# A two-layer transformer kernel on one core: routing by a search for the two largest, routing of the second step done earlier, and the first chain of layer 1 out of PSUM

## What is computed

```python
x = L0_attn_x                                  # (16, 256, 128)
xn = layernorm(x)
x = x + attn0(xn) + ffn0(xn)
xn = layernorm(x)
x = x + attn1(xn) + ffn1(xn)

def attn0(x):     # 8 heads of 64, windows of 128 and their neighbours
    xn = layernorm(x) * ln_g + ln_b
    qk, v = split(xn @ w_qkv.T)                # keys and queries are the same
    q, k = rotate(bucket(qk)), rotate(look_around(bucket(qk)))
    return softmax(mask(q @ k.T)) @ look_around(bucket(v)) @ w_out.T

def ffn0(x):      # a shared expert and 8 routed ones of 256, 2 per token
    p = softmax(x @ router_w + router_b)
    topk_probs, topk_idx = top_k(p, 2)
    weights = scatter(topk_idx, topk_probs)
    mixed = sum_e weights[:, e] * (gelu(x @ rw1[e] + rb1[e]) @ rw2[e] + rb2[e])
    return gelu(x @ sw1 + sb1) @ sw2 + sb2 + mixed

def attn1(x):     # gated unit without softmax, over the whole sequence
    u, v, base = split(silu((layernorm(x) * ln_w + ln_b) @ uv_w.T + uv_b))
    q, k = rope(base * gamma[0] + beta[0]), rope(base * gamma[1] + beta[1])
    return (u * (relu(q @ k.T / sqrt(128) + bias) ** 2 @ v)) @ o_w.T + o_b

def ffn1(x):      # a shared expert and routed ones
    return routed(x, 8 of 32 experts of 64, out of the best 2 of 4 groups) + shared(x)
```

## Time and profile before

| | before |
|---|---|
| median of 3 runs | 1052.2 us |
| lowest and highest | 1051.57 and 1052.24 us |
| profiled execution, its own time | 1052.27 us |
| span of the profile | 1051.0 us |
| TensorE busy | 997.6 us |
| VectorE, ScalarE, POOL busy | 680.0, 506.6, 425.9 us |
| mean granted TensorE clock | 0.99 of full |

### The profile page before, as it was taken

How to read it: one execution, slowest core, us unless ns; L and a number is a source line. 1 busy time by engine, 2 the same in 40 slices (tenths; PEclk the granted TensorE clock), 3 DMA queues, 4 the chain that set the end, 5 groups by cost and what they waited for, 6 DMA issues and landing times.

```text
span 1051.0 us, 13320 instructions
## 1 busy us (share of the span) xinstructions
PE 997.6 (95%) x4440; PEld 623.3 (59%) x4440; DVE 680.0 (65%) x1501; ACT 506.6 (48%) x1192; POOL 425.9 (41%) x336
## 2 busy tenths in 40 slices
PE   5799889799999999999999999999999999999998
PEld 2455556367555666556665675656665566656655
DVE  4846755849766587647766497665976557724933
ACT  3463573252654546454474525635266453644222
POOL 4737315454036520655108350175303652044433
PEclk9899989999999999999999999999999999999999
DMA  7140220060232302332032310323022220242061
GB/s 263 29 144 1 93 60 1 6 147 21 70 86 71 80 1 92 84 82 49 11 108 59 90 41 11 121 65 89 21 89 67 68 73 8 84 104 80 21 143 40
DMA packets 34565, 72.78 MB, mean 69 GB/s; under 512 B 4545, under 2 KB 5313, under 8 KB 34113
## 3 DMA queue, kind: packets, MB, share of 16 engines
q1 hardware_dynamic: 33072, 69.03, 24.0%
q10 hardware_dynamic: 1424, 2.90, 0.8%
HBM read 69.04 MB, written 2.88 MB: 68 GB/s over the span
## 4 chain that ended last, share of the span: by engine, by line
PE 88%; DVE 6%; issue 3%; ACT 3%; DMA 0%; POOL 0%; DVEq 0%; ACTq 0%; POOLq 0%
PE ps L692 11%; PE ps L589 11%; PE ps L453 9%; PE ps L455 9%; PE ps L454 9%; PE ps L501 6%; PE ps L514 6%; PE ps L526 5%; PE ps L667 3%; PE ps L477 3%; PE ps L484 2%; PE ps L597 2%; PE ps L638 2%; PE ps L448 1%; PE ps L493 1%
## 5 line engine op out<-in xcount | busy, mean ns | idle before, releaser
L1091 ACT ACTIVATE wide<-ps 128x512 f32<-128x512 f32 x136 | 80.9, 595 | 221.4 <-PE ps L455 220.8
L1022 ACT ACTIVATE pw<-ps,w_cols 128x512 f32<-128x512 f32 x144 | 98.8, 687 | 111.2 <-PE ps L455 109.5
L1771 POOL TENSOR_TENSOR atc<-atc,wide 128x512 f32<-128x512 f32 x64 | 82.8, 1294 | 156.4 <-DVE atc L1519 156.4
L982 ACT ACTIVATE pw<-ps,nmax 128x256 f32<-128x256 f32 x256 | 118.1, 470 | 52.8 <-DVE nmax L1319 52.7
L589 PE MATMUL ps<-pw,w_w 128*128 128x512 f32 x288 | 138.1, 603 | 0.0
L1753 POOL TENSOR_TENSOR kr<-qks,w_rope 128x512 f32<-128x512 f32 x32 | 43.5, 1360 | 194.8 <-DVE qks L1299 194.8
L1328 DVE COPY pt<-ps 128x512 f32<-128x512 f32 x128 | 85.7, 681 | 32.7 <-PE ps L514 31.7
L1390 DVE SCALAR_TENSOR_TENSOR pt<-ps,w_cols,wb 128x512 f32<-128x512 f32 x64 | 47.8, 747 | 88.0 <-PE ps L589 73.6
L514 PE MATMUL ps<-ident,pw 128*128 128x128 f32 x512 | 83.7, 287 | 21.3 <-DVE pt L1328 13.1
L1319 DVE TENSOR_REDUCE nmax<-ps 128x4 f32<-128x1024 f32 (+1 forms) x80 | 79.3, 1009 | 36.0 <-PE ps L501 35.9
L514 PEld LDWEIGHTS ps<-ident,pw 128*128 128x128 f32 x512 | 55.9, 142 | 60.9 <-issue 39.9
(11 more groups left out here) (221 smaller groups left out, 2098.3 us busy)
## 6 DMA issues: line engine op xcount, KB each, us to landing
wb<-scratch SPq DMA_DIRECT2D x128, 256.0 KB, 4.0
wb<-scratch SPq DMA_DIRECT2D x32, 512.0 KB, 5.4
wide<-scratch SPq DMA_DIRECT2D x16, 512.0 KB, 6.0
xin<-in_x SPq DMA_DIRECT2D x8, 256.0 KB, 2.7
out<-wide SPq DMA_DIRECT2D x8, 256.0 KB, 2.1
w_w<-in_w ACTq DMA_DIRECT2D x1, 1152.0 KB, 11.0
wb<-in_w SPq DMA_DIRECT2D x1, 1152.0 KB, 12.4
w_ed<-in_ed SPq DMA_DIRECT2D x1, 1024.0 KB, 17.3
```

The costliest lines, as they stand in the source:

```text
L982: m = act.activation(pw[:, u % 2, j, :], ps[:, score_bank(u, par), qt * SEQ:(qt + 1) * SEQ], ACT.Exp, bias=nmax[:, u % 3, j:j + 1], scale= ...
L1022: act.activation(hid[:, n % 4, :], bank(UPS0[n % 2]), ACT.Gelu, bias=cols[:, C_B1 + 2 * e + c:C_B1 + 2 * e + c + 1], scale=1.0).then_inc(* ...
L1771: pool.tensor_tensor(hh[h], hh[h], sgl[:, (c + 1) % 3, :], ALU.mult).then_inc(*HH_POOL.one)
```

## The change

1. **Search instead of rank.** `route0_top` takes the place of `route0_rank`: one `max` per tile (the 8 logits in falling order, `top0`), a memset that overwrites places 2 to 7 with a number no logit has, and one `match_replace` per tile, which marks the two places that hold the two largest. `route0_less` takes the maximum from `top0`, so its own reduction goes. `zc` is no longer scratch; the waits of the rank and of `z1_cols(0)` for it go. In step 0 the search stands behind round 1 of the attention, `route0_less` behind round 2, `exp0` and `route0_weights` in round 4, and the turning of the weights in round 5 or 6.
2. **The second step's routing one step early.** In `experts0(0)`, `y0_rows(1)`, `turn_y0(1)`, `y0_high(1)`, `y0_low(1)` and `logits0(1)` stand some calls earlier, so the logits come before `attention_out` and the search before `join0`. Two buffers `yc` make this possible: `columns0` and `columns1` choose one by step. At the head of `attention(1)`, `rows0(0)` on TensorE and `x1_rows(0)` and `variance1(0)` on VectorE move from before round 0 to its end, into a score bank; `shifts(1, 0)` moves to round 2, `z1_rows(0)` behind both exponentials of round 3.
3. **First chain out of PSUM.** `affine1(0)` writes to PSUM banks 6 and 2 (`affine`) and stands behind the gelus of the shared expert and of the first; `swap1` and `rope1_add` read there. In `experts0_and_chain1(1)` the order changes on all engines: the statistics of x of step 2 (`variance0(2)`, `shifts(0, 2)`, `power(0, 2)`) come earlier, `qk1` one expert's product later, `tanh1` before a gelu and not after `z0_cols`, the routing of layer 1 ahead of the rotation of step 2, the last two projections later.
4. **Key halves on POOL.** A new event `ROPED_K` for the key half. In step 2 the four adds of the key half are done by POOL (`rope_add_k`), not by VectorE.
5. **Start.** ScalarE makes `short_ident` as soon as `ident` is there (`IDENT`), where POOL did; so ScalarE's first activation no longer stands behind the first shift.

The steps from 2 on keep their order on all engines, but for the search in the place of the rank in `experts1`.

```diff
@@ buffers, banks
-        y0c, y1c = sb("y0c", [P, 2, TOK], F32R), sb("y1c", [P, 2, TOK], F32R)
+        yc = [sb("yc0", [P, 2, TOK], F32R), sb("yc1", [P, 2, TOK], F32R)]
...
+        def affine(s, i):
+
+            return qa1[:, i, :] if s else bank((6, 2)[i])
+
+        def columns0(s):
+
+            return yc[0 if s == 0 else 1]
+
+        def columns1(s):
+
+            return yc[1 if s == LAST else 0]
@@ pe_program, attention
-                if second:
-                    rows0(0, 7)
...
+                    if u == 0 and second:
+                        rows0(0, score_bank(0, 1))
...
-                    if u == 4 and first:
-                        turn_weights0(s, score_bank(4, 1))
+                    if u == 5 and first:
+                        turn_weights0(s, score_bank(5, 1))
@@ pe_program, experts0
+                if s == 0:
+                    turn_y0(n, 6)
                 down0(s, 5)
                 up0(s, 7)
                 if more:
-                    values(n, 1, 6)
-                    values(n, 2, 3)
+                    values(n, 1, 3)
+                    values(n, 2, 2)
+                if s == 0:
+                    logits0(n, 6)
                 down0(s, 6)
                 if more:
-                    values(n, 3, 6)
-                if s == 0:
-                    turn_y0(n, 2)
+                    values(n, 3, 3)
                 attention_out(s)
                 if s == 0:
-                    logits0(n, 3)
+                    turn_logits0(n, 6)
                     scores(n, 0)
                 down0(s, 7)
                 if s == 0:
-                    turn_logits0(n, 6)
                     scores(n, 1)
@@ pe_program, experts0_and_chain1
                 up0(s, 1)
+                down0(s, 0)
                 turn_y1(x, 3)
-                down0(s, 0)
+                up0(s, 2)
                 qk1(x, 0, 6)
                 qk1(x, 1, 2)
-                up0(s, 2)
@@ act_program, attention
                     v1_silu(0, 1)
-                    affine1(0)
                     gelu(s, E0)
                     gelu_half(s, 0, 0)
...
                 gelu_half(s, 0, 1)
+                if second:
+                    affine1(0)
@@ act_program, before the first step
-            w.wait_ge(*CONSTANTS.at(0))
+            w.wait_ge(*IDENT.at(0))
+            act.activation(short_ident[:, :], ident[:, :], ACT.Identity).then_inc(*SHORT_IDENT.one)
@@ dve_program
+            def route0_top(s):
+
+                for t in range(TILES):
+                    m = dve.max(top0[:, t, :], lg0[:, t, :])
+                own(m)
+                own(dve.memset(top0[:, :, 2:8], NONE))
+                for t in range(TILES):
+                    m = dve.match_replace(mr0[:, t, :], top0[:, t, :], lg0[:, t, :], TAKEN)
+                own(m)
 
             def route0_less(s):
-                own(dve.tensor_reduce(mx0[:, :], lg0[:, :, :], AX_X, ALU.max))
-                dve.tensor_tensor(lg0[:, :, :], lg0[:, :, :], spread(mx0[:, :], [(1, TILES), (0, E0)]),
+                dve.tensor_tensor(lg0[:, :, :], lg0[:, :, :], spread(top0[:, :, :], [(8, TILES), (0, E0)]),
@@ dve_program, rope_out
-                w.wait_ge(*TURNED_K.at(s, p))
-                dve.tensor_tensor(kr[:, p, :], kr[:, p, :], rtmp[:, h, :], ALU.add)
+                if s != 2:
+                    w.wait_ge(*TURNED_K.at(s, p))
+                    dve.tensor_tensor(kr[:, p, :], kr[:, p, :], rtmp[:, h, :], ALU.add).then_inc(*ROPED_K.one)
@@ pool_program, experts0_and_chain1
                 rope_turn(n, 0)
                 add0(s, 4)
+                rope_add_k(n, 0)
                 rope_turn(n, 1)
+                rope_add_k(n, 1)
```

More of the change, by code:

```diff
@@ L33 @@
 TAKEN = -3.0e38
+NONE = 3.0e38
 PAIR_SWAP = [i ^ 1 for i in range(32)]
@@ L943, in y0_high @@
                 w.wait_ge(*Y0_TURNED.at(s))
-                copy(y0c[:, 0, :], bank(k), Y0_HIGH)
+                copy(columns0(s)[:, 0, :], bank(k), Y0_HIGH)
             def y1_cols(s, k):
@@ L1105, in attention @@
                         exp0(s)
-                    if u == 2 and first:
+                    if u == 4 and first:
                         exp0(s)
@@ L1109, in attention @@
                         wt0_copy(s, score_bank(2, 1))
-                        z1_rows(0)
                     if u == 4 and s > 1:
                         wt0_copy(s, score_bank(3, 1))
-                    if u == 5 and first:
-                        wt0_copy(s, score_bank(4, 1))
+                    if u == 6 and first:
+                        wt0_copy(s, score_bank(5, 1))
                     if u == 5 and second:
@@ L1117, in attention @@
                     exps(s, u, 1)
+                    if u == 3 and second:
+                        z1_rows(0)
                 if second:
@@ L1477, in rope1_add @@
                 w.wait_ge(LOADED["rope1"], 16)
-                own(dve.tensor_tensor(seqs(qa1[:, i, :]), seqs(qa1[:, i, :]), table(rope1, 0), ALU.mult))
+                own(dve.tensor_tensor(seqs(affine(s, i)), seqs(affine(s, i)), table(rope1, 0), ALU.mult))
                 w.wait_ge(*TURNED1.at(s, i))
-                dve.tensor_tensor(qa1[:, i, :], qa1[:, i, :], qs1[:, i, :], ALU.add).then_inc(*ROPED1.one)
+                dve.tensor_tensor(qa1[:, i, :], affine(s, i), qs1[:, i, :], ALU.add).then_inc(*ROPED1.one)
             r = relb[:, :, :]
@@ L1553, in attention @@
                         route0_weights(s)
+                    if u == 1 and first:
+                        route0_top(s)
                     if u == 2 and first:
+                        route0_less(s)
+                    if u == 4 and first:
                         route0_weights(s)
@@ L1588, in experts0 @@
                     rope_out(n, 3, 2)
+                if first:
+                    y0_low(n, 6)
                 weigh0(s, 5)
```

148 lines of the change are left out of this document (75 added, 73 removed).

## The result

| | before | after |
|---|---|---|
| median of the runs shown | 1051.9 us (1051.4 to 1052.2, 4 runs) | **1027.2 us** (1025.6 to 1029.0, 4 runs) |
| ratio, 95% interval | 1 | 0.9766 (0.9749 to 0.9783) |
| profiled execution, its span | 1052.3, 1051.0 | 1027.4, 1026.1 |
| TensorE, VectorE busy | 997.6, 680.0 | 990.7, 656.5 |

The account below looks back on a forecast made before the run. TensorE, busy 997.6 of 1051.0 us, was taken to bound the kernel, with nearly all its idle time before 262 us. Terms 1.3 + 7.7 + 4.9 + 13.5 = 27.4 us, from 1052.27 to 1024.9 us; range 1021.5 to 1030.

Parts of the forecast that it names:

- the granted clock is under 0.7 behind 20 us: Sign of being wrong: TensorE's granted clock under 0.7 anywhere behind 20 us.
- rival (a): First chain: the clock falls at the remaining 2.3 us wait, 2.8 us not won, 1027.7 us; chance 0.18.
- Start: Kernel start: ScalarE's table load runs while x is on its way, first rows earlier; 1.3 us won.
- Step 0's attention: Step 0: the shorter search, a round later, removes TensorE's 5.3 us wait and the clock loss behind it; 7.7 us won.
- no wait over 1 us: Sign of being right: no wait of TensorE over 1 us in step 0's attention.
- Head of the second step: Second step's attention: TensorE's 3.5 us wait for x and its clock loss go, 2.7 us of waits remain; 4.9 us won.
- x uses a score bank ... nobody waits for it at once: Head of the second step: x leaves bank 7 for a score bank, so TensorE's 3.5 us wait goes.
- First chain: Second step's experts and first chain: 3.8 us wait becomes 2.3, other waits and clock losses go; 13.5 us won.
- 2.3 is nearer to 1.6, so I take full clock: First chain: the clock stays full behind the remaining 2.3 us wait, as after 1.6 us before; 2.8 us won.
- Rival (b): First chain: POOL and VectorE get in each other's way, TensorE waits 2.6 us, 1027.5 us; chance 0.12.
- Later steps: Search replaces the rank in six steps, no TensorE wait names it: 0 us; prediction fails if these steps change length.
- the steps from 2 on ... can neither add to the gain nor take it back: Steps from 2 on are bound by TensorE's own work, so their share of the gain is 0 us.

Follow-up runs that it names:

- The runs of search and rank: Kernel before with the search at the rank's old places, 1044.8 us; changed kernel with the old rank at the search's new places, 1033.5 us.
- the first run: Kernel before with the search in place of the rank, at the rank's old places: 1044.8 us, ratio 0.9923.

## Why the prediction was right, and where it was off

The direction, the size and the range held, and most of the mechanism. Two steps of it did not: full clock behind the wait that remained, and later steps that keep their length. With these fell two of the prediction's own signs of being wrong: the granted clock is under 0.7 behind 20 us (0.50 from 138 to 140 us), and the later steps changed their length. The median of 1027.2 lies just outside the 1022 to 1027 that I had given the forecast, and nearer to the 1027.7 of rival (a) than to 1024.9. Point by point:

**Start**, 1.3 forecast, 1.1 won: right. The changed kernel's rows start at 8.38 us, not at about 8.2. The rest is x, which landed 0.3 us later in this execution than in the one before the change; it landed up to 0.4 us earlier in others. The run with the start alone won 1.0 and shows 1.30 us from the load to the next activation again. By the 2.66 us of the Trainium skill (ScalarE: Activation LUTs, What ACT_TABLE_LOAD costs) the term would have been estimated at 2.7; the runs do not bear that out.

**Step 0's attention**, 7.7 and 7.8: right, with the search at 1.16 us (34.81 to 35.97) where I had 1.4. The sign "no wait over 1 us" held, and the clock is full throughout. The runs of search and rank show that the length decides the long wait here; the later place hides 0.5 us of a rank.

**Head of the second step**, 4.9 and 4.2. I had left waits of 1.2 and 1.5 us. The first is there at 1.19, the other is 0.92, and three more of 0.26 to 0.42 are there too, 3.1 in all where I had 2.7. This is 0.4 of the 0.7 too many; the rest is not traced. The step "x uses a score bank ... nobody waits for it at once" was true, but it won nothing: the old bank is 1.1 us better. The gain came from the new order at this place; with it even the old rank costs nothing here. That it is the routing's move, and not that of `z1_rows` or of the shifts, is likely but not shown.

**First chain**, 13.5 and 12.4. The list of waits held: 2.36 us left, where I had 2.3, none for `wr`, `er`, `qr` or `vr`; `wr` is finished 7.3 us ahead (173.60 against 180.86), I had some 9. The step that failed is "2.3 is nearer to 1.6, so I take full clock". It was not a matter of nearer: the clock falls behind this wait in some executions and not in others, four of six here. This costs 1.7 us where it happens, less than the 2.8 of rival (a), which took over the loss behind the 3.8 us wait of before. The other terms of the chain were slightly too small: in the changed kernel's execution with full clock, the case that the term was made for, the chain won 14.0 us (174.28 before, 160.23 after), 0.5 more than forecast; which term this is was not traced. Rival (b) had its cause right and its effect wrong. POOL is in VectorE's way in the first chain (1.10 us instead of 0.29, above), but TensorE doesn't wait for it: the run with the key adds on VectorE shows no difference.

**Later steps**, 0 and -0.6. The step "the steps from 2 on ... can neither add to the gain nor take it back" failed, and with it the sign that they keep their length. I had looked for the cost of the search there and found none, rightly. I passed over the value products' banks, which the change alters for all steps and not for the opening alone. The product moved to bank 2 waits 0.74 us for that bank's last reader, and each step is 0.16 us longer for it. (The section on the change says that the later steps keep their order but for the search. That is so, but they do not keep their banks.)

The sum's 2.5 us too many are thus 0.2 at the start, 0.7 at the head, 1.1 in the first chain (1.6 for the clock, less the 0.5 that the chain won beyond the forecast) and 0.6 later, less 0.1 in step 0. That the total came this close is in part luck, since two small errors in the first chain and in step 0 stand against the others.

## What to carry to other kernels

When a change renames a buffer or a bank in code that all steps share, read the steady stretch too: 0.16 us that repeat in every step add up to 0.65 here. When a blocked piece is moved off a path, look at what it had been covering; the transposes for x had filled a table load. And a wait that leaves the clock alone in one trace may not do so in the next: profile twice before a clock effect is put into a sum as all or nothing, and prefer to fill such a wait with work.

## What the runs showed of the hardware

The clock's fall is not a function of the wait in front of it alone. Behind 3.5 us and more it fell in every profile (before, and the runs with 3.7, 3.8, 4.1 and 4.8 us; the start apart). Behind 2.36 us at one place it fell in four profiles of six; behind 2.39 us at another (the first run) it did not. Behind 1.6 us in the second step before the change it did not either. In the last step two waits stand 16 us apart. Behind that for `wr`, 1.5 us long, the clock stayed full in all 13 profiles that have it. Behind the shorter one, for `atc`, it fell at 1.34 and at 1.25 us, and stayed full in the twelve others, with 0.90 to 1.21 us. What else decides stays open: the rows at 984 us have the DMA engines full (share 1.05), but so had the execution that kept its clock (share 0.97 at 136.85 us).

VectorE's product of two SBUF operands took 1.28 us beside a POOL instruction of 1.28 us and 0.29 without one. The search's instructions kept their length: each replace took 0.15 us and the four maxima 0.34 to 0.37 together, both in step 0 with POOL busy (34.81 to 35.97) and at the head of the second step with POOL idle (93.75 to 94.95). The Trainium skill (SBUF — State Buffer, Who interferes with whom) says that a VectorE instruction with two inputs in SBUF contends with a GpSimd one that reads SBUF; the trace agrees (1.28 against 0.29 us). The exchange of two neighbours in VectorE's order was so worth 1.9 us, of which 0.7 was the instruction that was moved and 1.0 the product that became shorter.
